# Routed experts on forty tiles of sorted rows in place of every expert on every token

## What is computed

```python
def ffn(x):                                   # x: layer-normed, 2048 x 128
    shared = (silu(x @ shared_gate.T) * (x @ shared_up.T)) @ shared_down.T     # hidden width 256
    probs = sigmoid(x @ router_w.T + routing_bias)                             # 8 experts
    scores, idx = top_k(probs, 2); scores = scores / scores.sum(-1)
    w = zeros(2048, 8); w[t, idx] += scores
    g = silu(einsum('th,ehi->tei', x, gate_w)); u = einsum('th,ehi->tei', x, up_w)
    return shared + einsum('tei,eih,te->th', g * u, down_w, w)
x = x + 0.5 * ffn(layernorm(x))
x = x + attention(layernorm(x))
x = x + 0.5 * ffn(layernorm(x))
```

## Time and profile before

| | us |
|---|---|
| median of 3 runs | 536.9 |
| lowest and highest run | 536.04, 538.03 |
| span of the profiled execution | 535.4 |
| PE busy in it | 470.2 (88%) |
| DVE busy in it | 447.8 (84%) |
| ACT busy in it | 298.4 (56%) |
| POOL busy in it | 171.4 (32%) |

### The profile page before, as it was taken

How to read it: one execution, slowest core, us unless ns; L and a number is a source line. 1 busy time by engine, 2 the same in 40 slices (tenths; PEclk the granted TensorE clock), 3 DMA queues, 4 the chain that set the end, 5 groups by cost and what they waited for, 6 DMA issues and landing times.

```text
span 535.4 us, 12227 instructions
## 1 busy us (share of the span) xinstructions
PE 470.2 (88%) x3847; PEld 311.4 (58%) x3847; DVE 447.8 (84%) x1155; ACT 298.4 (56%) x651; POOL 171.4 (32%) x199
## 2 busy tenths in 40 slices
PE   1778899999999668889989989985789999999996
PEld 0344566666666445766766766764455666666664
DVE  3699999999999837897888888876598999999997
ACT  3544555555555665657656656643555555555552
POOL 2999950000000373555556555534000000000000
PEclk9999999999999898999999999996599999999999
DMA  6222000000000000000000000000000000000002
GB/s 202 89 61 81 1 0 0 0 0 0 0 1 1 1 1 0 2 1 1 0 0 0 0 0 0 0 1 1 2 1 2 0 0 0 0 0 0 0 0 78
DMA packets 6693, 7.04 MB, mean 13 GB/s; under 512 B 784, under 2 KB 5136, under 8 KB 6672
## 3 DMA queue, kind: packets, MB, share of 16 engines
q1 hardware_dynamic: 6528, 6.39, 3.8%
q10 hardware_dynamic: 144, 0.39, 0.2%
HBM read 5.73 MB, written 1.05 MB: 13 GB/s over the span
## 4 chain that ended last, share of the span: by engine, by line
PE 61%; DVE 19%; issue 10%; ACT 4%; POOL 3%; DMA 1%; DVEq 0%; POOLq 0%; ACTq 0%
PE bank L1106 15%; PE bank L1118 9%; PE bank L1120 9%; PE bank L1119 9%; DVE h L773 4%; PE bank L1283 4%; DVE q_heads L859 3%; PE bank L1155 2%; DVE h_lo L779 2%; ACT gate_s L300 2%; PE bank L1231 2%; PE bank L1157 2%; PE bank L1156 2%; DVE x L762 2%; DVE stats L671 1%
## 5 line engine op out<-in xcount | busy, mean ns | idle before, releaser
L305 ACT ACTIVATE h_hi<-h 128x512 f16<-128x512 f32 x144 | 90.7, 630 | 135.4 <-DVE h L773 135.4
L773 DVE SCALAR_TENSOR_TENSOR h<-bank,gate_s 128x512 f32<-128x512 f32 x144 | 99.4, 690 | 27.2 <-ACT gate_s L300 21.7
L1106 PE MATMUL bank<-w_hi,h_hi 128*128 (+1 forms) x576 | 105.8, 220 | 15.7 <-DVE h_lo L779 10.9
L1118 PE MATMUL bank<-xt_hi,w_hi 128*128 128x512 f16 x288 | 110.7, 385 | 0.1
L1119 PE MATMUL bank<-xt_hi,w_lo 128*128 128x512 f16 x288 | 110.7, 384 | 0.0
L1120 PE MATMUL bank<-xt_lo,w_hi 128*128 128x512 f16 x288 | 110.7, 384 | 0.0
L1106 PE MATMUL bank<-w_hi,h_lo 128*128 (+1 forms) x576 | 105.0, 220 | 0.0
L1106 PE MATMUL bank<-w_lo,h_hi 128*128 (+1 forms) x576 | 105.0, 219 | 0.0
L779 DVE TENSOR_TENSOR h_lo<-h,h_hi 128x512 f16<-128x512 f32 x144 | 103.4, 718 | 0.1
L762 DVE SCALAR_TENSOR_TENSOR x<-bank,wts,x 128x128 f32<-128x128 f32 x288 | 86.4, 343 | 1.3 <-PE bank L1106 0.9
L300 ACT ACTIVATE gate_s<-bank 128x512 f32<-128x512 f32 x144 | 83.6, 581 | 0.0
(11 more groups left out here) (170 smaller groups left out, 881.6 us busy)
## 6 DMA issues: line engine op xcount, KB each, us to landing
wf<-in_w_ffn SPq DMA_DIRECT2D x8, 384.0 KB, 3.0
x<-in_x SPq DMA_DIRECT2D x4, 256.0 KB, 5.2
out_dram<-x SPq DMA_DIRECT2D x4, 256.0 KB, 2.3
cst<-in_consts SPq DMA_DIRECT2D x1, 454.0 KB, 5.6
wf<-in_w_ffn ACTq DMA_DIRECT2D x1, 384.0 KB, 4.5
wqkvg<-in_w_qkvg SPq DMA_DIRECT2D x1, 256.0 KB, 3.2
wslots<-in_w_slots SPq DMA_DIRECT2D x1, 256.0 KB, 3.1
wo<-in_w_out SPq DMA_DIRECT2D x1, 64.0 KB, 2.9
```

What stands on the lines that cost most here:

```text
L305: act.activation(h_hi[:, g, ih, :], h32[:, ih, :], ACT.Copy).then_inc(hhi_done, 1)
L773: nc.vector.scalar_tensor_tensor(h32[:, ih, :], up_ps[ih][:, :], HS / (XS * WS), gate_s[:, ih, :], ALU.mult, ALU.mult).then_inc(hmul_done, 1)
L1106: i = mm(dst, hp[:, g, ih, c * P:(c + 1) * P], wcols(wp, e, at, D), start=(k == 0), stop=(k == 3 * IH - 1))
L1118: mm(ps[:, :], wcols(w_hi, e, at, P), xt_hi[:, ts], start=True, stop=False)
```

## The change

The shared expert still runs on all tokens, as eight units. The routed experts run only on the tokens that chose them:

- The normed rows are split into high and low before they are turned (`xrow`, one row of 256 fp16 values and the token's number), and turned by PE in fp16. A second copy of each row is made, since each token goes to two experts.
- After the router DVE and PE count, for each of the 4096 choices, how many of its expert come before it. An expert's rows begin at a multiple of 128, so 4096 rows and 8 partly filled tiles fit in `TILES` = 40 tiles always. The place of a row is `slot_of`, the expert of a tile `expert_of`.
- POOL writes the rows to their places in DRAM (`dispatch`, 32 indirect DMAs of 128 rows), over rows of padding that SP has written (`pad`).
- SP brings them back with five transposing DMAs of 1024 rows, features on partitions (`xst`), and then the token numbers (`y_at`).
- PE runs 20 units of two tiles, with the expert's weights addressed by a value that it loads (`value_load`). Gate and up are then twelve matmuls of 128 columns each; a unit has 36 matmuls of 128 columns. ACT copies the down sums to `y_slot` (four buffers).
- POOL writes each tile's 128 rows to DRAM in token order (`send`, 40 indirect DMAs). SP loads them (`load_y`), and DVE adds the two rows of each token to x, times its share (`combine`).
- The weights' splits move from POOL to ACT and DVE, between the shared units. Some buffers of the attention share memory with the new ones; its instructions stay.

The core of the diff, with the functions of SP, POOL, DVE and PE that the prediction speaks of:

```diff
-BY_DVE = (1, 1, 2)
-SPF = NG * E
+BY_DVE = 1
+TOPK = 2
+UG = IH * NG
+PAIR = 2
+TILES = TOPK * NC + ER
+NP = TILES // PAIR
+UF = UG + NP
+SLOTS = TILES * P
+LOAD = 8
+NL = TILES // LOAD
+ROW = 2 * D + 8
+AT_ID = 2 * D
+PAD_ID = 2 * TOPK * T
+YB = 4
+HR = 4
...
+            def load_slots(f):
+
+                sp.wait_ge(dispatched, 16 * TOPK * NC * (f + 1))
+                if f:
+                    sp.wait_ge(up_done, UF)
+                for b in range(NL):
+                    rows = slice(b * LOAD * P, (b + 1) * LOAD * P)
+                    sp.dma_start_transpose(xst[:, :, rows], slots_d[f][rows, 0:2 * D]).then_inc(slots_loaded[b], 16)
+                for b in range(NL):
+                    rows = slice(b * LOAD * P, (b + 1) * LOAD * P)
+                    sp.dma_start(y_at[:, b * LOAD:(b + 1) * LOAD].bitcast(F16).rearrange("p (t r) -> p t r", r=2),
+                                 slots_d[f][rows, AT_ID:AT_ID + 2].rearrange("(t p) r -> p t r", p=P)).then_inc(y_at_loaded[b], 16)
+
+            def load_y(f):
+
+                for b in range(YB):
+                    sp.wait_ge(y_sent[b], 32 * (NP // YB) * (f + 1))
+                if f:
+                    sp.wait_ge(combined, NG)
+                for g in range(NG):
+                    for k in range(TOPK):
+                        sp.dma_start(y_tok[:, k, g * GT:(g + 1) * GT, :],
+                                     y_d[f][k * T + g * GW:k * T + (g + 1) * GW, :].rearrange("(c p) d -> p c d", p=P)).then_inc(y_loaded[g], 16)
+
...
+            load_slots(0)
+            pad(1)
+            load_y(0)
+            load_slots(1)
+            load_y(1)
...
+            def dispatch(f):
+
+                pool.wait_ge(padded[f], 16 * NL)
+                pool.wait_ge(row_done, NG * (f + 1))
+                pool.wait_ge(slots_known, f + 1)
+                for c in range(NC):
+                    for k in range(TOPK):
+                        nc.gpsimd.indirect_dma_start(slots_d[f], bass.IndirectOffsetOnAxis(slot_of[:, k, c:c + 1], 0),
+                                                     xrow[:, k, c, :], None, bounds_check=SLOTS - 1, oob_is_err=False).then_inc(dispatched, 16)
+
+            def send(f):
+
+                for s in range(NP):
+                    pool.wait_ge(y_copied, NP * f + s + 1)
+                    for j in range(PAIR):
+                        t = PAIR * s + j
+                        if t % LOAD == 0:
+                            pool.wait_ge(y_at_loaded[t // LOAD], 16 * (f + 1))
+                        nc.gpsimd.indirect_dma_start(y_d[f], bass.IndirectOffsetOnAxis(y_at[:, t:t + 1], 0),
+                                                     y_slot[:, s % YB, j, :], None, bounds_check=TOPK * T - 1,
+                                                     oob_is_err=False).then_inc(y_sent[s % YB], 16)
+
...
+            def row_again(f, g):
+
+                cs = slice(g * GT, (g + 1) * GT)
+                dve.wait_ge(row_lo_done, NG * f + g + 1)
+                nc.vector.tensor_copy(xrow[:, 1, cs, 0:2 * D], xrow[:, 0, cs, 0:2 * D]).then_inc(row_done, 1)
...
-            def add_half(f, e, g, j):
-
-                s = SPF * f + NG * e + g
-                dve.wait_ge(down_done, 2 * s + j + 1)
-                for c in range(2 * j, 2 * j + 2):
-                    t = g * GT + c
-                    i = nc.vector.scalar_tensor_tensor(x[:, t, :], down_ps[j][:, c % 2 * P:(c % 2 + 1) * P],
-                                                       wts[:, t, e:e + 1] if isinstance(e, int) else wts[:, t, bass.ds(e, 1)],
-                                                       x[:, t, :], ALU.mult, ALU.add)
-                i.then_inc(added, 1)
...
+            def combine(f, g):
+
+                dve.wait_ge(y_loaded[g], 32 * (f + 1))
+                dve.wait_ge(share_done, f + 1)
+                dve.wait_ge(added, UG * (f + 1))
+                for k, done in enumerate((combine_step, combined)):
+                    if k:
+                        dve.wait_ge(combine_step, NG * f + g + 1)
+                    for c in range(g * GT, (g + 1) * GT):
+                        i = nc.vector.scalar_tensor_tensor(x[:, c, :], y_tok[:, k, c, :], share[:, c, k:k + 1], x[:, c, :],
+                                                           ALU.mult, ALU.add)
+                    i.then_inc(done, 1)
 
...
+            def unit_slots(f, s, experts):
+
+                n = UF * f + UG + s
+                pe.wait_ge(hmul_done, n - 1)
+                if PAIR * s % LOAD == 0:
+                    pe.wait_ge(slots_loaded[PAIR * s // LOAD], 16 * (f + 1))
+                for base, ps, done in ((0, gate_ps[s % 2], gate_done), (I, up_ps[s % 2], up_done)):
+                    for j, e in enumerate(experts):
+                        js = slice((PAIR * s + j) * P, (PAIR * s + j + 1) * P)
+                        for ih in range(IH):
+                            at, dst = base + ih * P, ps[:, (j * IH + ih) * P:(j * IH + ih + 1) * P]
+                            mm(dst, wcols(w_hi, e, at, P), xst[:, 0, js], start=True, stop=False)
+                            mm(dst, wcols(w_lo, e, at, P), xst[:, 0, js], start=False, stop=False)
+                            i = mm(dst, wcols(w_hi, e, at, P), xst[:, 1, js], start=False, stop=True)
+                    i.then_inc(done, 1)
+
...
+            def down_slots(f, s, experts):
+
+                u = UG + s
+                pe.wait_ge(hlo_done, UF * f + u + 1)
+                if s >= 2:
+                    pe.wait_ge(y_copied, NP * f + s - 1)
+                else:
+                    pe.wait_ge(added, UG * (f + 1))
...
+                unit_shared(f, 0)
+                unit_shared(f, 1)
+                rank(f)
+                for u in range(2, UG):
+                    unit_shared(f, u)
+                    if u >= 3:
+                        down_shared(f, u - 3)
+                for d in range(UG - 3, UG):
+                    down_shared(f, d)
                 if f == 0:
-                    pe.wait_ge(wlo_done, E - 1)
...
+                    pe.wait_ge(elo_done, E)
+                pe.wait_ge(experts_known, f + 1)
+                held = []
+                for s in range(NP):
+                    held.append([bass.ds(pe.value_load(expert_of[0:1, PAIR * s + j:PAIR * s + j + 1], min_val=1, max_val=ER), 1) for j in range(PAIR)])
+                    unit_slots(f, s, held[s])
+                    if s >= 2:
+                        down_slots(f, s - 2, held[s - 2])
+                for s in range(NP - 2, NP):
+                    down_slots(f, s, held[s])
...
-            def step(f, e, before):
-
-                for g in range(NG):
-                    unit(f, e, g, 0, False)
-                    down_half(f, e if g >= 2 else before, (g - 2) % NG, 1)
-                    unit(f, e, g, 1, False)
-                    down_half(f, e if g >= 1 else before, (g - 1) % NG, 0)
+                    pe.wait_ge(elo_done, E)
```

701 lines of the change are left out of this document (425 added, 276 removed).

## The result

The changed kernel takes **582.4 us** (median of 4 runs, 581.5 to 583.7) against 536.9 (536.0 to 538.0, 4 runs beside them): the ratio is 1.083, with a 95% interval of 1.079 to 1.087. It is slower by 45 us, where the prediction had it 15 us faster (and gave 0.45 to slower).

What follows compares the result with a forecast made beforehand. The prediction took TensorE as the bound, with 173 us of PE work removable; exposed routing, dispatch, transposes, tiles and return left gains of 8.1 and 6.5 us, a 520.8 us span and 522.3 us in all, range 480 to 605.

Steps and rivals of the forecast that it cites:

- The views and the bound before: Profile readings before the change: TensorE bounds the kernel, VectorE close behind; less PE work offers 173 us for both feed-forwards.
- a unit is 3.1 us: Expert tiles on PE: array 1.98 us a unit, but sequencer issue, register operations and two loads make it 3.1 us.
- +49.6: Error, both feed-forwards together, of the step from dispatched rows landed to all rows returned, predicted at 78.3 us each.
- PE sets the end of the tiles: Rival, expert tiles: low PE clock or TENSOR_LOADs of 0.95 us give 4.0 us a unit, 549 us in all; chance 0.08.
- tile units that take over 3.5 us on PE while POOL waits for `y_copied`: Sign in the changed kernel's profile, at the expert tiles, that would show the forecast wrong.
- Indirect DMA at 1.2 us: POOL's dispatch and return: each of 144 indirect DMAs takes 1.2 us; the change is worth nothing from 1.30 us.
- the rival in which the 144 issues pay it one after another: POOL's indirect DMAs: completion not overlapped, 0.95 us more each, 137 us above the forecast; no separate chance given.
- Transposes at 4.5 us: SP's five transposing DMAs after dispatch: 4.5 us for each 512 KB, the middle of 2.5 and 6.4; five are 22.5 us.
- my cheap case: Rival, all cheap: indirect DMA 1.04 us and transpose 2.5 us, 500 to 480 us in all; chance 0.15.
- the 12.6: Step from the router's sums to the slot numbers in each feed-forward: 12.6 us, including 2.0 for four exposed copies.
- the forecast's own 500 to 540: Range in us of the likeliest case, indirect DMA 1.05 to 1.3 us and transpose 3 to 6 us; chance 0.40.
- dearer POOL issues or transposes: Two rivals: indirect DMA at 1.6 us, 580 us, chance 0.25; transposes at 12 us each, 597 us, chance 0.12.

Runs made afterwards that it cites:

- ahead: Changed kernel with all 40 expert numbers of a feed-forward loaded into PE's registers before the first sorted rows, not two per unit: 532.0 us, ratio 0.989 to the kernel before.
- static: Changed kernel with fixed expert numbers for the 40 tiles instead of the router's, so no loads or register operations for them on PE: 518.5 us.

## Why the prediction was wrong, point by point

- **The views and the bound before** were read rightly: PE's busy time falls from 470 to 363 us, DVE's from 448 to 298 and ACT's from 298 to 230, so the work did go.
- **The step that failed is the PE tile unit, "a unit is 3.1 us".** Its terms: product issue 1.0, register operations 0.9 + 0.2, loads 1.0. The loads with their own register operations were about right (1.2 against 2 x 0.66 = 1.3). The 24 register operations of the products were not: I multiplied their row's duration, 0.046 + 0.032, by their count, 0.9 us; they take 24 x 0.091 = 2.2. In this trace the duration of such a row is not the time until the next instruction of that sequencer goes. The Trainium skill, Perfetto Trace Analysis, section "Sequencer-only Instruction (DRAIN, etc)", says so: the profiler reports the execution alone, and fetch, decode and the push of the semaphore are not in it. The trace agrees: 0.30 + 0.15 + 0.02 us of rows for a load that takes 0.66. A unit is 1.4 us dearer than forecast, and there are 40.
- **What it did to the sum.** The prediction had POOL ahead of PE by 4 us, so a unit above 3.3 us turned the order round, and from there each 0.1 us of a unit is 2 us a feed-forward. At 4.5 us the 20 units alone take nearly 90 us, and the tiles with the return 104.6 and 101.6 us. That makes the whole +49.6, with the cheaper transposes already in it.
- **The rival "PE sets the end of the tiles" was the one that came true**, with 0.08 as its chance and 549 us as its price. Its place was right. Its mechanism (the low clock, or dearer loads) was not, and so neither its 4.0 us a unit nor its chance. The list of things that would show the forecast wrong did name it: "tile units that take over 3.5 us on PE while POOL waits for `y_copied`".
- **Indirect DMA at 1.2 us**: measured 1.28 mostly, 1.32 and 1.29 on average over the two dispatches, which is +4.3 us for both; the landing took 2.3 us as assumed. It was the cost that I had ranked first and it was nearly right. The DMAs do overlap: the median from issue to landing is 2.2 us, and the next starts 1.28 us later. Against the figure of about 2.0 us each by the Trainium skill's page DMA: Bandwidth & Descriptors, section "Anatomy of one DMA — SWDGE (gpsimd) path", this trace shows that as latency, not as pace: the rival in which the 144 issues pay it one after another did not come.
- **Transposes at 4.5 us**: measured 12.67 / 5 = 2.53 us from one issue to the next for 512 KB, the price of my cheap case and below the 3 to 6 us of the forecast; in `ahead` POOL has its first addresses 97.80 - 81.28 = 16.5 us after the dispatch has landed, not 28.0. This gain of 11.5 us a feed-forward was lost behind PE. The Trainium skill's 350 to 400 GB/s for a transposing DMA (Advanced Engine Details and Errata, "X-Bar Transpose (TRN2)") is not reached here: 512 KB in 2.53 us is 207 GB/s.
- **Router and attention**: the sums come 3.5 and 4.8 us later, since the split now stands in front of the turn. In the chain of the first norm each group passes ACT's `xrow` (L385, 1.66 us) and DVE's (L880, 0.69 us) before PE may turn it. The four copies of 128x1024, for which I took 2.0 us inside the 12.6, cost nothing there: DVE is through with them and then idle for 1.45 us, waiting for PE, before it reads the sums, in both feed-forwards. That cost stood in the sum under the wrong name and too small.
- **With the unit as predicted** the forecast can be tried: `ahead` has a unit of 3.15 us, and takes 532.0, within the forecast's own 500 to 540. PE and not POOL still ends it, by the 6.8 us between 157.12 and `static`'s last return at 150.29.
- **The range** (480 to 605) held 582.4, but by luck: its upper part stood for dearer POOL issues or transposes, and neither came. The forecast's own range, 500 to 540, did not hold it.

## What to carry to other kernels

Where a value from memory chooses the operand, count the instructions of the sequencer and price them by the distance between two of them in a trace, not by the duration of their row: here a register operation took 0.09 us and a load 0.66, and 24 and 2 of them made a unit of 2.0 us into one of 4.5. Move such loads in one block into a time in which the engine waits anyway, and prefer forms in which one address serves several products. If an engine that was the bound loses work, ask again for all of its parts, the sequencer too, how far it is from becoming the bound once more.
